# Image 2's expert sums move from TensorE to GpSimd, and two other moves in the tail of a fused attention and expert kernel

## The chip, the cores and the metric

One core of one Trainium2 chip runs the whole program. The metric is device time in microseconds (us) of one execution. TensorE (PE) multiplies matrices, VectorE (DVE), ScalarE (ACT) and GpSimd (POOL) work element by element, SyncE (SP) issues DMAs.

## What is computed

Four images of 64 channels and 1024 positions pass through an attention with projections, then a second attention on the normalized tokens, then a mixture of eight experts of which each token uses the two best. Cut to the last part, which the change touches:

```python
def _L1_ffn_ref(x, router_w, router_b, expert_w, expert_b):       # K = 2
    router_probs = jax.nn.softmax(x @ router_w + router_b, axis=-1)
    top_p, top_i = jax.lax.top_k(router_probs, K)
    top_p = top_p / jnp.sum(top_p, axis=-1, keepdims=True)
    expert_out = jnp.einsum('bnd,edc->bnec', x, expert_w) + expert_b
    gathered = jnp.take_along_axis(expert_out, top_i[..., None], axis=2)
    return jnp.einsum('bnk,bnkc->bnc', top_p, gathered)

t = t + _L1_attn_ref(_ln_t(t))
t = t + _L1_ffn_ref(_ln_t(t), router_w, router_b, expert_w, expert_b)
x = _from_tokens(t, x)
```

The kernel computes all eight experts for every token and multiplies each by a gate that is zero for six of them.

## The kernel before

Every engine has its own program, written out by hand in the order in which it runs; semaphores are the only link between them. Images 0 to 3 are staggered: while one image is in its first attention, the one ahead of it is in its second, and the experts of an earlier one run in between. Matmul results go into a ring of three PSUM buffers, in the order of the table ORDER; acc1 and acc2 are two further PSUM banks in which sums grow.

Tokens lie on partitions, 128 at a time, eight tiles to an image; two tiles are a pair, so an image has four pairs, g = 0 to 3. The steps that matter here, for image b:

- tokens2 (L1201, L1206) on VectorE turns the second attention's result into tok2; norm_stats (L1160 to L1171) takes the statistics of it; rstd on GpSimd (L370) raises the variances to the power -0.5; normalize2 (L1211) makes wn, the normalized tokens.
- w_transposed (L581) on TensorE turns wn, ScalarE rounds it into w_hi (L935), VectorE keeps the rest in w_lo (L1216); route (L594) makes the logits; top2 (L1224 to L1255) on VectorE picks two experts per token in some twenty small steps, each waiting for the one ahead, and ends in gate.
- experts (L605) multiplies a pair by all eight expert matrices into the ring; weigh_experts (L1266) multiplies that by the gates into prod, whose pair g is 128 x 1024: 8 experts x 2 tiles x 64 channels.
- For images 0 and 1 GpSimd adds the eight experts of a pair in three halving steps, sum_pair (L382, L384, L386: half, quart, ysum), and then residual and bias.
- For images 2 and 3, the tail, TensorE does the adding: start_sums (L624, L628) puts the turned tok2 and the turned expert bias into acc1 or acc2, and add_experts (L635) adds experts to them, each by one product with the identity, which turns it as well. Pair 0 of image 2 is added as eight experts; of pairs 1 to 3, and of pairs 0 to 2 of image 3, GpSimd first adds the upper four experts to the lower four in place (L421), so that TensorE adds four; the last pair is halved twice by VectorE (L1412, L1414) and TensorE adds two.
- GpSimd begins these in-place additions only behind a wait for s_w, that is for the wn of image 3.
- gates_transposed (L614) turns the gates, ScalarE copies them to gate_t (L943), and the bias products of start_sums wait for that. ScalarE copies the finished sums to ob (L1101 for image 2, L1105 and L1107 for the two halves of image 3), and SyncE stores them (L324, L330).

TensorE's order in the tail of before is: experts(2,1), experts(2,2), start_sums(2), add_experts(2,0), w_transposed(3), experts(2,3), route(3), experts(3,0) to (3,2), add_experts(2,1) to (2,3) with gates_transposed(3) ahead of the last of them, experts(3,3), start_sums(3) for pairs 0 and 1, their add_experts, start_sums(3) for pairs 2 and 3, and their add_experts.

Of the kernel before, what the change touches and what calls it, by code (L numbers as in the profile page):

```python
# [17 lines left out]
ALU = mybir.AluOpType  # L18
# [6 lines left out]
P = 128  # L25
B, C, N, M, E = 4, 64, 1024, 32, 8
CHUNK = 512
T = N // P
# [55 lines left out]
def build(nc, x, wq, wk, wv, wo, rw, rb, ew, eb, out):  # L84
    ctx = ExitStack()
    with ctx:
# [10 lines left out]
        ident = sb("ident", [P, P])  # L97
# [41 lines left out]
        ob = two("ob", [P, CHUNK])  # L139
# [29 lines left out]
        prod = sb("prod", [P, T // 2, E, 2, C])  # L169
        half = sb("half", [P, E // 2, 2, C])  # L170
        quart = sb("quart", [P, E // 4, 2, C])
        ysum = sb("ysum", [P, T, C])
# [124 lines left out]
        @block.sync  # L297
        def _(sp):
            def load_x(b):
                for h in range(2):  # L300
                    sp.dma_start(xin[h * C:(h + 1) * C, b, :], x[b].rearrange("c h w -> c (h w)")).then_inc(s_x[b], 16)

            first = x[0].rearrange("c h w -> c (h w)")
            for part in range(2):
                for h in range(2):
                    sp.dma_start(xin[h * C:(h + 1) * C, 0, chunk(part)], first[:, chunk(part)]).then_inc(s_x0[part], 16)
            sp.wait_ge(s_const, 1)
            for h in range(2):
                sp.dma_start(wo4[:, 2 * h, :], wo).then_inc(s_wol, 16)
            load_x(1)  # L310
            for h in range(2):
                sp.dma_start(e_in[h * C:(h + 1) * C, :, :], ew.rearrange("e d c -> d e c")).then_inc(s_ew, 16)
                sp.dma_start(r_in[h * C:(h + 1) * C, :], rw).then_inc(s_ew, 16)
            sp.dma_start(rb_all[:, :], rb.rearrange("(a e) -> a e", a=1).to_broadcast([P, E])).then_inc(s_ew, 16)
            for t in range(T):
                sp.dma_start(eb_in[t * E:(t + 1) * E, :], eb).then_inc(s_ew, 16)
            for b in range(2, B):
                load_x(b)

            flat_out = out.rearrange("b c h w -> (b c) (h w)")  # L320
            for b in range(B - 1):
                sp.wait_ge(s_ob, b + 1)
                for h in range(2):
                    sp.dma_start(flat_out[b * C:(b + 1) * C, chunk(h)], ob[b % 2][h * C:(h + 1) * C, :]).then_inc(s_out[b % 2], 16)  # L324
            b = B - 1
            for half_sum in range(2):
                sp.wait_ge(s_ob, B + half_sum)
                lo, hi = half_sum * CHUNK // 2, (half_sum + 1) * CHUNK // 2
                for h in range(2):
                    sp.dma_start(flat_out[b * C:(b + 1) * C, h * CHUNK + lo:h * CHUNK + hi],  # L330
                                 ob[b % 2][h * C:(h + 1) * C, lo:hi]).then_inc(s_out[b % 2], 16)
            sp.wait_ge(s_out[0], 2 * 32)
            sp.wait_ge(s_out[1], 3 * 32)
# [3 lines left out]
        def _(pool):  # L337
# [30 lines left out]
            def rstd(b, s_ve, s_rs, sm):  # L368
                pool.wait_ge(s_ve, b + 1)
                pool.tensor_tensor(sm[:, 3, :], sm[:, 2, :], minus_half[:, :], ALU.pow).then_inc(s_rs, 1)  # L370
                pool.wait_ge(s_rs, b + 1)
# [40 lines left out]
            rstd(3, s_ve1, s_rs1, sm1)  # L412
            experts(1)
            rstd(2, s_ve2, s_rs2, sm2)
            rstd(3, s_ve2, s_rs2, sm2)

            pool.wait_ge(s_w, B)
            for b, pairs in ((2, (1, 2, 3)), (3, (0, 1, 2))):
                for n, g in enumerate(pairs):
                    pool.wait_ge(s_prod, (T // 2) * b + g + 1)  # L420
                    pool.tensor_tensor(prod[:, g, 0:E // 2], prod[:, g, 0:E // 2], prod[:, g, E // 2:E],  # L421
                                       ALU.add).then_inc(s_half, 1)


        @block.tensor
        def _(pe):
# [194 lines left out]
            def start_sums(b, tiles, bank):  # L621

                for t in tiles:
                    pe.matmul(bank[:, t % len(tiles) * P:(t % len(tiles) + 1) * P],  # L624
                              tok2[b % 2][:, 2 * t:2 * t + 2, :].rearrange("p h c -> p (h c)"), ident[:, :],
                              start=(t == tiles[0]), stop=False)
                for t in tiles:
                    pe.matmul(bank[:, t % len(tiles) * P:(t % len(tiles) + 1) * P],  # L628
                              eb_blk[:, 2 * t:2 * t + 2, :].rearrange("p h c -> p (h c)"), gate_t[:, :],
                              start=False, stop=False)  # L630

            def add_experts(b, t, n, where, last):

                for e in range(n):
                    mm = pe.matmul(where, prod[:, t, e].rearrange("p h c -> p (h c)"), ident[:, :],  # L635
                                   start=False, stop=(last and e == n - 1))
                mm.then_inc(s_sums, 1)
# [214 lines left out]
            pe.wait_ge(s_tk2, 3)  # L852
            pe.wait_ge(s_gt, 3)
            start_sums(2, range(4), acc1)
            pe.wait_ge(s_prod, (T // 2) * 2 + 1)
            add_experts(2, 0, E, acc1[:, 0:P], False)
            w_transposed(3)
            experts(2, 3)
            route(3)
            experts(3, 0)  # L860
            experts(3, 1)
            experts(3, 2)
            for t in range(1, 4):
                pe.wait_ge(s_half, (T // 2) * 2 + t)
                add_experts(2, t, E // 2, acc1[:, t * P:(t + 1) * P], t == 3)
                if t == 2:
                    gates_transposed(3)
            experts(3, 3)
            pe.wait_ge(s_ob, 3)
            pe.wait_ge(s_tk2, B)  # L870
            pe.wait_ge(s_gt, B)
            start_sums(3, range(2), acc1)
            for t in range(2):
                pe.wait_ge(s_half, (T // 2) * 2 + 4 + t)
                add_experts(3, t, E // 2, acc1[:, t * P:(t + 1) * P], t == 1)
            start_sums(3, range(2, 4), acc2)
            pe.wait_ge(s_half, (T // 2) * 2 + 6)
            add_experts(3, 2, E // 2, acc2[:, 0:P], False)
            pe.wait_ge(s_tail_v, 2)
            add_experts(3, 3, E // 4, acc2[:, P:2 * P], True)  # L880
# [4 lines left out]
        def _(act):  # L885
# [219 lines left out]
            act.activation(ob[b % 2][:, 0:CHUNK // 2], acc1[:, 0:CHUNK // 2], ACT.Copy).then_inc(s_ob, 1)  # L1105
            act.wait_ge(s_sums, 8)
            act.activation(ob[b % 2][:, CHUNK // 2:CHUNK], acc2[:, 0:CHUNK // 2], ACT.Copy).then_inc(s_ob, 1)  # L1107


        @block.vector  # L1110
        def _(dve):
# [145 lines left out]
            def weigh_experts(b, g):  # L1257
                buf = filled(dve, f"e{g}", b)
                if g == 0:
                    dve.wait_ge(s_gate, b + 1)  # L1260
                if b in (1, 2):
                    dve.wait_ge(s_half, (T // 2) * (b - 1) + g + 1)
                if b == 3:
                    dve.wait_ge(s_sums, g + 1)
                gates = gate[b % 2][:, 2 * g:2 * g + 2, :].unsqueeze(3).to_broadcast([P, 2, E, C])
                dve.tensor_tensor(prod[:, g].rearrange("p e h c -> p h e c"), buf.rearrange("p h (e c) -> p h e c", c=C),  # L1266
                                  gates, ALU.mult).then_inc(s_prod, 1)
# [171 lines left out]
```

## Time and profile before

| what | value |
|---|---|
| device time, median of 3 runs | 212.69 us (212.67 to 213.76) |
| span of the profiled execution, first to last instruction | 211.2 us |
| what lies around the span (median less span) | some 1.5 us |
| TensorE busy | 197.3 us (93%) |
| VectorE busy | 144.4 us (68%) |
| ScalarE busy | 107.0 us (51%) |
| GpSimd busy | 62.0 us (29%) |
| TensorE clock granted over the span | 1.000 |

The page's busy rows by slices show TensorE at 7 to 9 tenths in nearly every slice, and GpSimd at 0 in nearly half of them; shares over the span say little about the last 25 us, though, where single steps wait for each other. The chain of waits says which they were. In the timeline a row gives start, duration, engine, line, operation, names, shapes and count, and in brackets how long the engine had been idle and who released it.

### The profile page before, as it was taken

To read this page: it belongs to the slowest core of one execution; us is meant where nothing else is said; L and a number is where in the kernel's file an instruction comes from. 1 tells how busy PE (TensorE), PEld (TensorE's weight loads), DVE (VectorE), ACT (ScalarE), POOL (GpSimd) and SP (SyncE) were. 2 spreads that over 40 slices of the span, in tenths; PEclk is the share of its full clock that TensorE was granted. 3 is DMA by queue.
4 is the path that set the end of the run, shared out by engine and by line. 5 is a ranking of instruction groups with operands and counts; after the bars stand their busy time and mean duration, and the time that the engine had idled before them with its cause. 6 is when DMAs were issued, how large, how long until landed. Compare 5 with 4: busy or idle time off the path is not lost.

```text
span 211.2 us, 3049 instructions
## 1 busy us (share of the span) xinstructions
PE 197.3 (93%) x1131; PEld 100.3 (47%) x1131; DVE 144.4 (68%) x359; ACT 107.0 (51%) x164; POOL 62.0 (29%) x75
## 2 busy tenths in 40 slices
PE   7999899899999899998989999899999999899993
PEld 2647443363734335453433545334435333387882
DVE  3889867978545994576489864827785362898980
ACT  3532776458655455576365636756555776301010
POOL 8140040403000300003003269710277770016270
PEclk9999999999999999999999999999999999999999
DMA  3853000000000000000000000020000002000021
GB/s 110 152 129 73 3 0 0 0 2 3 2 0 0 0 0 3 0 0 3 0 0 2 3 0 2 0 53 0 0 0 3 0 0 51 0 3 0 0 53 50
DMA packets 3502, 3.69 MB, mean 17 GB/s; under 512 B 2208, under 2 KB 2464, under 8 KB 3488
## 3 DMA queue, kind: packets, MB, share of 16 engines
q1 hardware_dynamic: 3248, 3.45, 7.2%
q8 instruction: 9, 0.15, 0.3%
q10 hardware_dynamic: 240, 0.05, 0.1%
q14 instruction: 5, 0.04, 0.1%
HBM read 2.45 MB, written 1.05 MB: 17 GB/s over the span
## 4 chain that ended last, share of the span: by engine, by line
PE 64%; DVE 26%; POOL 4%; issue 3%; ACT 2%; DVEq 0%; POOLq 0%
PE acc L494 19%; PE ring L558 9%; DVE rowmax L1127 8%; PE ring L605 6%; PE ring L487 5%; PE ring L469 5%; POOL sm L370 4%; PE acc L635 3%; PE acc L641 2%; PE ring L531 2%; DVE stats L1160 2%; PE ring L542 2%; PE ring L594 2%; DVE tok L1206 2%; PE ring L458 1%
## 5 line engine op out<-in xcount | busy, mean ns | idle before, releaser
L914 ACT ACTIVATE prob<-ring,shift 128x1024 f32<-128x1024 f32 x32 | 35.6, 1112 | 23.6 <-PE ring L558 23.3
L1127 DVE TENSOR_REDUCE rowmax<-ring 128x1 f32<-128x1024 f32 x32 | 38.1, 1219 | 12.5 <-PE ring L469 12.4
L370 POOL TENSOR_TENSOR sm<-sm,minus_half 128x8 f32<-128x8 f32 x8 | 15.8, 1974 | 99.7 <-DVE sm L1170 99.7
L911 ACT ACTIVATE prob<-ring 128x1024 f32<-128x1024 f32 x32 | 32.0, 1024 | 18.1 <-PE ring L487 18.0
L494 PE MATMUL acc<-prob,u 128*64 128x512 f32 x128 | 31.2, 606 | 0.2 <-ACT prob L914 0.2
L494 PE MATMUL acc<-prob,val 128*64 128x512 f32 x128 | 31.0, 605 | 0.0
L1266 DVE TENSOR_TENSOR prod<-ring,gate 128x1024 f32<-128x1024 f32 x16 | 19.3, 1220 | 6.8 <-PE ring L605 6.7
L487 PE MATMUL ring<-kst,qst 98*128 98x512 f32 x64 | 21.4, 425 | 1.1 <-DVE kst L1124 0.5
L469 PE MATMUL ring<-qst,kst 96*128 96x512 f32 x64 | 21.7, 429 | 0.7 <-DVE rowmax L1127 0.4
L558 PE MATMUL ring<-zsw,zst 64*128 64x512 f16 x64 | 19.4, 376 | 0.0
L558 PE MATMUL ring<-zst,zsw 64*128 64x512 f16 x64 | 19.2, 376 | 0.0
L487 PEld LDWEIGHTS ring<-kst,qst 98*128 98x128 f32 x64 | 10.4, 188 | 11.7 <-ACT prob L911 5.4
L494 PEld LDWEIGHTS acc<-prob,u 128*64 128x64 f32 x128 | 7.7, 136 | 15.6 <-issue 12.9
L494 PEld LDWEIGHTS acc<-prob,val 128*64 128x64 f32 x128 | 7.7, 136 | 15.2 <-issue 12.0
L469 PEld LDWEIGHTS ring<-qst,kst 96*128 96x128 f32 x64 | 10.2, 189 | 10.0 <-DVE rowmax L1127 4.0
L376 POOL TENSOR_TENSOR xst<-xin,xst 64x1024 fp32r<-64x1024 f32 x3 | 7.1, 2374 | 25.8 <-ACT xst L888 25.8
L382 POOL TENSOR_TENSOR half<-prod 128x512 f32<-128x512 f32 x8 | 10.6, 1322 | 8.4 <-DVE prod L1266 8.2
L558 PE MATMUL ring<-zst 64*128 64x512 f16 x32 | 12.3, 386 | 0.7 <-DVE rowmax L1127 0.4
L605 PE MATMUL ring<-e,w_hi 64*128 64x512 f32 x64 | 12.4, 443 | 0.0
L558 PE MATMUL ring<-zsw 64*128 64x512 f16 x32 | 12.4, 386 | 0.0
L605 PE MATMUL ring<-e,w_lo 64*128 64x512 f32 x64 | 10.9, 394 | 0.0
L641 PE MATMUL acc<-filler 128*128 128x512 f16 x21 | 7.9, 513 | 1.5 <-DVE filler L1270 1.5
(160 smaller groups left out, 323.8 us busy)
## 6 DMA issues: line engine op xcount, KB each, us to landing
xin<-in_x SPq DMA_DIRECT2D x6, 256.0 KB, 4.2
out<-ob SPq DMA_DIRECT2D x6, 128.0 KB, 2.4
xin<-in_x SPq DMA_DIRECT2D x4, 128.0 KB, 2.8
e_in<-in_L_ffn_expert_w SPq DMA_DIRECT2D x2, 128.0 KB
out<-ob SPq DMA_DIRECT2D x4, 64.0 KB, 2.0
eb_in<-in_L_ffn_expert_b SPq DMA_DIRECT2D x8, 2.0 KB
wo<-in_L_conv_wo SPq DMA_DIRECT2D x2, 8.0 KB, 2.2
r_in<-in_L_ffn_router_w SPq DMA_DIRECT2D x2, 2.0 KB
```

Of the source, the lines that this page charges most:

```text
L370: pool.tensor_tensor(sm[:, 3, :], sm[:, 2, :], minus_half[:, :], ALU.pow).then_inc(s_rs, 1)
L382: pool.tensor_tensor(half[:, :, :, :], p[:, 0:E // 2], p[:, E // 2:E], ALU.add).then_inc(s_half, 1)
L469: mm = pe.matmul(buf[:, h, :], kst[home][0:ROW, col(tile):col(tile) + P], qst[home][0:ROW, h * CHUNK:(h + 1) * CHUNK], start=True, stop=True)
L487: mm = pe.matmul(buf[:, h, :], qst[home][0:ROW + 2, col(j):col(j) + P], kst[home][0:ROW + 2, h * CHUNK:(h + 1) * CHUNK], start=True, stop= ...
L494: mm = pe.matmul(acc[h * C:(h + 1) * C, :], stationary[:, j, :], prob[:, j % DEEP, h * CHUNK:(h + 1) * CHUNK], start=(j == 0), stop=(j == ...
L558: mm = pe.matmul(buf[:, h, :], held[h][rows, col(j):col(j) + P], moving[h][rows, h * CHUNK:(h + 1) * CHUNK], start=(n == 0), stop=(n == 2))
L605: mm = pe.matmul(buf[:, h, :], w[rows, g * P:(g + 1) * P], e[rows, :], start=(n == 0), stop=(n == 3))
L641: pe.matmul(bank[:, :], filler[:, 0:P], filler[:, :], start=True, stop=True)
L911: act.activation(prob1[:, j % DEEP, :], flat(filled(act, f"st{j}", b)), ACT.Exp).then_inc(s_p1, 1)
L914: act.activation(prob2[:, j % DEEP, :], flat(filled(act, f"s{j}", b)), ACT.Exp, bias=shift[:, :], accum_out=rsum2[b % 2][:, j:j + 1]).then ...
L1127: dve.tensor_reduce(rowmax[:, tile:tile + 1], flat(filled(dve, f"mx{tile}", b)), AX.X, ALU.max).then_inc(s_mx, 1)
L1266: dve.tensor_tensor(prod[:, g].rearrange("p e h c -> p h e c"), buf.rearrange("p h (e c) -> p h e c", c=C), gates, ALU.mult).then_inc(s_pr ...
```

## The change

GpSimd's program: sum_pair for pair 0 of image 2 is put ahead of the last rstd, that of image 3, and sum_pair for pairs 1 to 3 behind it, in place of the three in-place additions of image 2; the wait for s_w is gone. The in-place additions for image 3 stay. GpSimd's end of program before, then after; names are those of the tiles above, sm is the statistics:

```order
L395 TENSOR_TENSOR y<-yres,ybias 128x512 [waits out_ready,ybias_ready,pool_step]
L370 TENSOR_TENSOR sm<-sm,minus_half 128x8 [waits var2_ready]
L370 TENSOR_TENSOR sm<-sm,minus_half 128x8 [waits var2_ready,rstd2_ready]
L421 TENSOR_TENSOR prod<-prod 128x512 [waits prods_ready,w_ready,rstd2_ready]
L421 TENSOR_TENSOR prod<-prod 128x512 [waits prods_ready] x5
```

```order
L370 TENSOR_TENSOR sm<-sm,minus_half 128x8 [waits var2_ready]
L382 TENSOR_TENSOR half<-prod 128x512 [waits prods_ready,rstd2_ready]
L384 TENSOR_TENSOR quart<-half 128x256 [waits prods_used]
L386 TENSOR_TENSOR ysum<-quart 128x128 [waits tree_step]
L370 TENSOR_TENSOR sm<-sm,minus_half 128x8 [waits var2_ready,tree_step]
L382 TENSOR_TENSOR half<-prod 128x512 [waits prods_ready,rstd2_ready]
L384 TENSOR_TENSOR quart<-half 128x256 [waits prods_used]
L386 TENSOR_TENSOR ysum<-quart 128x128 [waits tree_step]
L382 TENSOR_TENSOR half<-prod 128x512 [waits prods_ready,tree_step]
```

One sum_pair now stands between the two L370 of images 2 and 3, and three follow the second one with no wait for wn.

TensorE's program: add_experts(2,0) and the three other add_experts of image 2 are gone; a new add_sums adds the four ysum pairs, one product each, behind experts(3,2). gates_transposed(3) comes behind them, then a wait for gate_t and start_sums(3) for pairs 2 and 3 into acc2, and only then experts(3,3). TensorE from image 2's adding to image 3's first pair, before, then after:

```order
L635 MATMUL acc1<-ident,prod 128x128 [waits prods_used]
L635 MATMUL acc1<-ident,prod 128x128 x3
L614 MATMUL acc2<-ident,gate_1 128x128 [waits gates_ready,att2_read]
L635 MATMUL acc1<-ident,prod 128x128 [waits prods_used]
L635 MATMUL acc1<-ident,prod 128x128 x3
L605 MATMUL ring<-e1,w_hi_1 128x512 [waits prods_ready]
...
L624 MATMUL acc1<-ident,tok2_1 128x128 [waits gates_transposed,tok2_ready,out_ready]
```

```order
L636 MATMUL acc1<-ident,ysum 128x128 [waits tree_step] x4
L615 MATMUL acc2<-ident,gate_1 128x128 [waits gates_ready,att2_read]
L625 MATMUL acc2<-ident,tok2_1 128x128 [waits gates_transposed,tok2_ready]
L625 MATMUL acc2<-ident,tok2_1 128x128
L629 MATMUL acc2<-gate_t,eb_blk 128x128 x2
L606 MATMUL ring<-e1,w_hi_1 128x512 [waits prods_ready]
...
L625 MATMUL acc1<-ident,tok2_1 128x128 [waits out_ready]
```

The products for acc2 moved from behind image 3's first two pairs to ahead of experts(3,3), and with them the wait for gate_t.

VectorE's order is the same; weigh_experts of image 3 now waits for GpSimd's first halving of the same pair of image 2, where it waited for TensorE's adding of it. Of the last four stores SyncE issues three; ScalarE issues the last, of the lower half of the last sums, behind its own copy. The diff:

```diff
@@ sync: last stores @@
-                for h in range(2):
+                for h in range(2 - half_sum):
                     sp.dma_start(flat_out[b * C:(b + 1) * C, h * CHUNK + lo:h * CHUNK + hi],
@@ gpsimd: end of program @@
             rstd(2, s_ve2, s_rs2, sm2)
+            sum_pair(2, 0)
             rstd(3, s_ve2, s_rs2, sm2)
-            pool.wait_ge(s_w, B)
-            for b, pairs in ((2, (1, 2, 3)), (3, (0, 1, 2))):
-                for n, g in enumerate(pairs):
-                    pool.wait_ge(s_prod, (T // 2) * b + g + 1)
-                    pool.tensor_tensor(prod[:, g, 0:E // 2], prod[:, g, 0:E // 2], prod[:, g, E // 2:E],
-                                       ALU.add).then_inc(s_half, 1)
+            for g in range(1, T // 2):
+                sum_pair(2, g)
+
+            for g in range(T // 2 - 1):
+                pool.wait_ge(s_prod, (T // 2) * 3 + g + 1)
+                pool.tensor_tensor(prod[:, g, 0:E // 2], prod[:, g, 0:E // 2], prod[:, g, E // 2:E],
+                                   ALU.add).then_inc(s_half, 1)
@@ tensor @@
+            def add_sums(b, t, bank):
+                pe.wait_ge(s_tree, ((T // 2) * b + t) * 2 + 2)
+                pe.matmul(bank[:, t * P:(t + 1) * P], ysum[:, 2 * t:2 * t + 2, :].rearrange("p h c -> p (h c)"), ident[:, :],
+                          start=False, stop=(t == T // 2 - 1)).then_inc(s_sums, 1)
             start_sums(2, range(4), acc1)
-            pe.wait_ge(s_prod, (T // 2) * 2 + 1)
-            add_experts(2, 0, E, acc1[:, 0:P], False)
             w_transposed(3)
...
             experts(3, 2)
-            for t in range(1, 4):
-                pe.wait_ge(s_half, (T // 2) * 2 + t)
-                add_experts(2, t, E // 2, acc1[:, t * P:(t + 1) * P], t == 3)
-                if t == 2:
-                    gates_transposed(3)
+            for t in range(T // 2):
+                add_sums(2, t, acc1)
+            gates_transposed(3)
+            pe.wait_ge(s_tk2, B)
+            pe.wait_ge(s_gt, B)
+            start_sums(3, range(2, 4), acc2)
             experts(3, 3)
             pe.wait_ge(s_ob, 3)
-            pe.wait_ge(s_tk2, B)
-            pe.wait_ge(s_gt, B)
             start_sums(3, range(2), acc1)
...
-            start_sums(3, range(2, 4), acc2)
@@ scalar: end of program @@
+            act.wait_ge(s_ob, B + 1)
+            act.dma_start(out[b].rearrange("c h w -> c (h w)")[:, CHUNK + CHUNK // 2:N],
+                          ob[b % 2][C:P, CHUNK // 2:CHUNK]).then_inc(s_out[b % 2], 16)
@@ vector: weigh_experts @@
-                if b in (1, 2):
+                if b:
                     dve.wait_ge(s_half, (T // 2) * (b - 1) + g + 1)
-                if b == 3:
-                    dve.wait_ge(s_sums, g + 1)
```

## Rows read from the trace of the kernel before

**Rows 1.** Chain of waits, the tail: start us, us, what.

```profile
186.30 0.70 DVE tok L1206
...
189.14 1.96 POOL sm L370
...
191.19 0.70 DVE wn L1211
...
192.03 0.63 PE ring L581 x4
...
193.78 0.99 PE ring L594 x8
...
207.80 0.38 ACT ob L1107
```

**Rows 2.** Timeline of GpSimd and VectorE near 133 us (start, duration, instruction).

```profile
132.31 1.28 POOL L390 TENSOR_TENSOR yres<-ysum,tok 128x512 f32<-128x512 f32 x1
132.36 1.78 DVE L1206 TENSOR_TENSOR tok<-odiv,tok 128x512 f32<-128x512 f32 x1
133.67 1.60 POOL L395 TENSOR_TENSOR y<-yres,ybias 128x512 f32<-128x512 f32 x1
```

**Rows 3.** Timeline, VectorE beside GpSimd near 128 us; ring lies in PSUM.

```profile
128.13 1.23 DVE L1266 TENSOR_TENSOR prod<-ring,gate 128x1024 f32<-128x1024 f32 x1 [0.44 <-PE ring L605]
128.25 0.73 POOL L384 TENSOR_TENSOR quart<-half 128x256 f32<-128x256 f32 x1
```

**Rows 4.** Timeline of GpSimd, one sum_pair of image 0.

```profile
119.90 1.29 POOL L382 TENSOR_TENSOR half<-prod 128x512 f32<-128x512 f32 x1 [3.68 <-DVE prod L1266]
121.27 0.74 POOL L384 TENSOR_TENSOR quart<-half 128x256 f32<-128x256 f32 x1
122.08 0.46 POOL L386 TENSOR_TENSOR ysum<-quart 128x128 f32<-128x128 f32 x1
```

**Rows 5.** Timeline of VectorE and GpSimd, routing of images 2 and 3.

```profile
181.43 0.17 DVE L1234 TENSOR_TENSOR gm<-top 128x8 f32<-128x8 f32 x1
...
184.44 1.23 DVE L1266 TENSOR_TENSOR prod<-ring,gate 128x1024 f32<-128x1024 f32 x1
...
191.80 1.22 DVE L1266 TENSOR_TENSOR prod<-ring,gate 128x1024 f32<-128x1024 f32 x1
...
195.23 1.30 POOL L421 TENSOR_TENSOR prod<-prod 128x512 f32<-128x512 f32 x1 [0.69 <-DVE prod L1266]
...
196.31 0.24 DVE L1234 TENSOR_TENSOR gm<-top 128x8 f32<-128x8 f32 x1
...
196.79 0.29 DVE L1239 TENSOR_TENSOR cand<-cand,ramp 128x128 f32<-128x128 f32 x1
...
199.07 0.22 DVE L1255 TENSOR_TENSOR gate<-pick 128x64 f32<-128x64 f32 x1
```

**Rows 6.** Timeline of TensorE and ScalarE, from the gates of image 3 on.

```profile
199.59 0.27 PE L614 MATMUL acc<-ident,gate 128*128 128x128 f32 x1
...
199.90 0.27 ACT L943 ACTIVATE gate_t<-acc 64x128 f32<-64x128 f32 x1 [3.10 <-PE acc L614]
...
200.69 0.73 PE L605 MATMUL ring<-e,w_hi 64*128 64x512 f32 x4
```

**Rows 7.** Timeline of SyncE's queue, the last two stores.

```profile
208.21 0.47 SPq L330 DMA_DIRECT2D out<-ob  x1
...
208.72 0.60 SPq L330 DMA_DIRECT2D out<-ob  x1
```

**Rows 8.** Timeline of TensorE: start of the program, longest wait, image 2's sums.

```profile
6.25 0.74 PE L445 MATMUL ring<-xst,w 128*96 128x512 f32 x1
...
7.70 0.39 PE L445 MATMUL ring<-xst,w 128*96 128x512 f32 x1
...
42.58 0.88 PE L478 MATMUL ring<-ident_r,nmax 128*98 128x128 f32 x8 [1.04 <-DVE nmax L1135]
...
188.61 1.16 PE L628 MATMUL acc<-gate_t,eb_blk 64*128 64x128 f32 x8
```

More of the change, by code:

```diff
@@ L862, in _ @@
             experts(3, 2)
-            for t in range(1, 4):
-                pe.wait_ge(s_half, (T // 2) * 2 + t)
-                add_experts(2, t, E // 2, acc1[:, t * P:(t + 1) * P], t == 3)
-                if t == 2:
-                    gates_transposed(3)
+            for t in range(T // 2):
[4 more added lines that the diff above has]
+            start_sums(3, range(2, 4), acc2)
             experts(3, 3)
             pe.wait_ge(s_ob, 3)
-            pe.wait_ge(s_tk2, B)
-            pe.wait_ge(s_gt, B)
             start_sums(3, range(2), acc1)
             for t in range(2):
-                pe.wait_ge(s_half, (T // 2) * 2 + 4 + t)
+                pe.wait_ge(s_half, (T // 2) * 3 + t + 1)
                 add_experts(3, t, E // 2, acc1[:, t * P:(t + 1) * P], t == 1)
-            start_sums(3, range(2, 4), acc2)
-            pe.wait_ge(s_half, (T // 2) * 2 + 6)
+            pe.wait_ge(s_half, (T // 2) * 3 + 3)
             add_experts(3, 2, E // 2, acc2[:, 0:P], False)
```

## The prediction

> **What bounds the kernel now.** I read the page, then the chain of waits over the last 25 us, then the timelines of VectorE and GpSimd there, and last of the other stretches in which these two work at once. The chain is to show that the end is not set by TensorE's amount of work. It runs from VectorE's tok2 of image 3 (186.30) over GpSimd's power (189.14 to 191.10) back to VectorE's wn (191.19 to 191.89), through the turn and the routing products on TensorE (192.03, 193.78) to VectorE's pick of two experts, which ends in the gates at 199.07 + 0.22 = 199.29 [rows 1, 5]. From there the last copy starts 8.51 later, at 207.80 [rows 1]. So I cost the change as: when do the gates come, and how long is the way from the gates to the end.
>
> The timelines are to show how VectorE and GpSimd hold each other up. Near 133 us GpSimd starts an addition at 132.31, VectorE starts tok2, with both inputs in SBUF, 0.05 later, and takes 1.78 instead of the 0.69 to 0.70 of the tail: it ends at 134.14, 0.55 after GpSimd's end at 133.59. GpSimd's next addition, started at 133.67 while tok2 still runs, takes 1.60 instead of 1.28, as if it had begun 0.15 into its time and waited until 134.14 [rows 1, 2]. One waits for the whole instruction of the other. A VectorE instruction that reads the ring in PSUM is free of it: 1.23 beside GpSimd's 0.73, both their usual times [rows 3, 4]. Small ones are not free: L1234 takes 0.17 alone, and 0.24 where GpSimd's addition ran until 196.53; it ended just behind that, at 196.55 [rows 5]. In the tail of before, GpSimd's additions stay away from tok2, stand behind wn by a wait, and overlap the pick of experts in one instruction alone.
>
> **The change part by part.** The sum is made on the profiled execution, whose span of 211.2 lies 1.5 under the median; I add differences to 212.69.
>
> *sum_pair(2,0), ahead of the power.* Image 2's first weighing ends at 184.44 + 1.23 = 185.67 [rows 5]. GpSimd follows a VectorE result after about 0.14 (as TensorE follows wn: 191.89 to 192.03 [rows 1]), so half runs from 185.81 to 187.09 [1.28, rows 2, 4]. tok2 of image 3 starts at 186.30 in the middle of that, reads two SBUF tiles, and would end 0.55 behind it, at 187.64, not at 187.00: **+0.65** on the chain. quart (0.74) and ysum (0.46) are done near 188.8, a microsecond ahead of the power, now at 189.79; so the power waits for VectorE and not for them, and that part costs nothing.
>
> *sum_pair(2,1), with the wait for wn gone.* The power ends at 191.74. GpSimd's own next instruction follows it after 0.08 (121.19 to 121.27 [rows 4]), at 191.82, since its products are long there; VectorE's wn follows after 0.09 to 0.10 (191.10 to 191.19 [rows 1]), at 191.84. If GpSimd gets in first, as it did with 0.05 of lead in [rows 2], half ends at 193.10 and wn at 193.65, where it would have ended at 192.54: **+1.11**. The bounds are 0 and 1.28; I take GpSimd first, though the lead is 0.02. On this the Trainium skill speaks against the change: its page SBUF — State Buffer, section Who interferes with whom, says that issue order decides who blocks, for the whole instruction. By that page the lead alone decides, however small, and the sum is the one made here; rows 2 agree with a lead of 0.05, and no row here shows one of 0.02.
>
> *sum_pair(2,2) and (2,3), beside the pick of experts.* All of VectorE is now 0.65 + 1.11 = 1.76 late. GpSimd's quart of pair 1 waits for wn and ends at 194.23, its ysum at 194.77. Pair 2's products come at 191.80 + 1.22 + 1.76 = 194.78 [rows 5]; a sum_pair takes 1.28 + 0.73 + 0.46 and two gaps of 0.08, 2.63 in all [rows 4], so pair 2 runs from 194.92 to 197.55 and pair 3 from 197.63: half to 198.91, quart from 198.99 to 199.72, ysum to 200.26. L1234 would start at 196.31 + 1.76 = 198.07; it ends behind half, at 198.94 instead of 198.31: +0.63. L1239 would then start at 196.79 + 1.76 + 0.63 = 199.18, and is held by quart until 199.72: 0.40, since an instruction comes 0.14 into its time before it is held. The later small steps fall behind ysum's end. So **+1.03**; the bounds are 0 and the 2.63 for which pair 3 keeps GpSimd busy, and the row nearest is L1234's own. The gates come at 199.29 + 0.65 + 1.11 + 1.03 = 202.08.
>
> *TensorE.* add_experts(2,0) goes from a place where TensorE next waits for wn anyway: nothing gained. The other three of image 2, twelve products, become four, and the last ysum, at 200.26, is there 1.8 ahead of the gates; so TensorE has added them and waits when the gates come, and what counts is the way from there. New: turn of the gates 0.14 after them, 0.31 to ScalarE's copy, 0.27 for that, 0.14 back [rows 1, 6] = 0.86; then the work that stood in before from experts(3,3) at 200.69 to the last copy at 207.80, 7.11 [rows 1, 6], the same instructions in another order, with the acc2 products first. 7.97 instead of 8.51: **-0.54**. The new wait of TensorE for gate_t holds experts(3,3) behind it, which VectorE's fourth weighing wants: experts(3,3) ends about 0.86 + 1.2 + 1.1 = 3.2 after the gates, and VectorE comes to that weighing after three of 1.22, at 3.7. So it hides, with 0.5 in hand.
>
> *The last store.* SyncE issues its second store 0.51 behind the first [rows 7]; by ScalarE's queue both are issued at once. **-0.45**, between -0.51 and, if ScalarE's landed later, +0.3.
>
> *weigh_experts' new wait* is for halvings that end by 198.91, ahead of the gates: nothing.
>
> Sum: 0.65 + 1.11 + 1.03 - 0.54 - 0.45 = +1.80, so 212.69 + 1.80 = **214.5**.
>
> **The rivals.** *VectorE gets in first at wn.* The handovers differ by 0.02 only. wn is then not held, GpSimd's half waits for it (0.55), pairs 2 and 3 come 0.15 later than above and the pick of experts 1.11 earlier, so that more of its steps meet them. Going through it as above, L1239, L1242 and L1244 are held, 1.48 in all: gates at 201.42, +1.14, 213.8.
>
> *GpSimd does not hold VectorE.* If tok2, wn and the pick kept their times, because the rows near 133 had another cause, only the gains stay: -0.99, 211.7. That is the other side: not slower. It decides at tok2 and wn, and [rows 2] speak against it, in both directions at once.
>
> *TensorE's clock falls.* With add_experts(2,0) gone TensorE has nothing from 188.61 + 1.16 = 189.77 to wn's turn at 193.79: 4.0 idle. The longest wait of TensorE once it was under way was 1.04 [rows 8], and the page grants the full clock over the span. What the lower level costs shows at the start: L445 takes 0.74 before, and 0.39 once the clock is up [rows 8]. The turn and the routing products on the chain take 0.63 + 0.99 [rows 1]; doubled, they add 1.6, and up to 3 if the experts' products behind them wait too. I take +1.7: 216.2. The Trainium skill's page TensorE: Matmul & The Clock Gate, section Part 1: The HAM clock gate, says that an idle TensorE falls back to 1.2 GHz and must work to get 2.4 GHz again; no row of before shows a fall inside the program.
>
> **How the numbers follow.** GpSimd first at wn, clock kept: 0.50, 214.5. VectorE first: 0.23, 213.8. Clock falls: 0.16, 216.2. No holding, or much less of it: 0.11, 211.7 to 212.6. About 0.5% (1.06) is what a measurement of this kernel can tell from no change. The likeliest gives 214.5. The range takes in the first two with their bounds and half of the third: 213.1 to 216.3. Faster by over 0.5%: half of the case without holding, 0.05. Within 0.5%, up to 213.75: the rest of that and nearly half of VectorE first, 0.16. Slower: 0.79.
>
> **What would show it.** In the profile after: tok2 of image 3 at 1.3 instead of 0.69, with GpSimd's half under it; wn at 1.8, or half at 1.8 instead; L1234, L1239 or L1242 at 0.5 to 1.0; GpSimd busy from 191.8 to 200.3; the gates near 202; last copy 8.0 behind them; two stores issued at once. Wrong would be: VectorE's steps at their old lengths with GpSimd busy beside them; the last copy nearer to 8.5 behind the gates, which takes the TensorE term away; a granted clock under 1 after 193.

## The result

The changed kernel took 216.72 us (median of 4 runs, 215.08 to 217.27) where the kernel before, run beside it, took 212.68 (212.54 to 213.76). The ratio is 1.0161 (95% interval 1.0119 to 1.0204), which on 212.68 is 216.1. Slower was forecast, at 214.5 within 213.1 to 216.3. So the side is right and the ratio's value lies in the range, but the median of the runs lies 0.4 above it. The case taken as likeliest is not the one that happened: the rival of the falling clock is, to which 0.16 was given, and the range holds the value because it was drawn to take in half of that rival. That is luck more than judgement. Where a ratio is given, runs more than 1.5% above the fastest of the same kernel are left out of it; this concerns two of the ten of e2_gap.

Of the profiled execution (216.46 us) the page shows first where to look. These are its span, its row of TensorE's busy share in 40 slices, and the clock granted in the same slices:

```profile
span 214.7 us, 2998 instructions
...
PE   7999899899999899998989999899999999839994
...
PEclk9999999999999999999999999999999999985799
```

A slice is 5.4 us. TensorE is busy for 3 tenths of the slice that begins near 188, and in the next two slices the clock stands at 5 and 7 tenths. Before, this row held a 9 in every slice. Over the whole span the four executions were granted 0.976, 0.992, 0.976 and 0.976; the second, at 0.992, is the one of 215.08.

The stretches around it, TensorE's column and the granted clock above all (stretch, length, busy time and instructions of each engine, clock, share of the DMA engines, GB/s):

```profile
189.00:191.00 2.00, 0.76 (x7) 0.57 (x6) 1.93 (x7) 0.00 (x0) 1.23 (x1) 1.00 0.00 0
191.50:192.00 0.50, 0.00 (x0) 0.00 (x0) 0.16 (x1) 0.00 (x0) 0.42 (x2) 0.57 0.00 0
192.00:193.00 1.00, 0.00 (x0) 0.00 (x0) 1.00 (x1) 0.00 (x0) 1.00 (x1) 0.50 0.00 0
193.80:201.60 7.80, 7.80 (x34) 6.00 (x36) 5.52 (x20) 0.81 (x2) 5.82 (x8) 0.50 0.00 0
202.00:202.50 0.50, 0.50 (x8) 0.39 (x6) 0.47 (x4) 0.00 (x0) 0.00 (x0) 1.00 0.00 0
```

The clock falls to its lower level, 1.2 of 2.4 GHz, near 191.6, while TensorE waits. It stays there until shortly before 202, although TensorE worked through 7.80 of the 7.80 us up to 201.60.

Now the steps. VectorE in the stretch of [rows 1, 5] (start, duration, line, instruction, idle time before it and who released it):

```profile
186.27 1.36 DVE L1212 TENSOR_TENSOR tok<-odiv,tok 128x512 f32<-128x512 f32 x1
...
191.84 1.78 DVE L1217 TENSOR_TENSOR wn<-cen,sm 128x512 f32<-128x512 f32 x1 [0.48 <-POOL sm L370]
...
199.97 0.42 DVE L1240 TENSOR_TENSOR gm<-top 128x8 f32<-128x8 f32 x1
...
200.62 0.43 DVE L1245 TENSOR_TENSOR cand<-cand,ramp 128x128 f32<-128x128 f32 x1
...
203.03 0.23 DVE L1261 TENSOR_TENSOR gate<-pick 128x64 f32<-128x64 f32 x1
```

GpSimd beside it:

```profile
185.79 1.30 POOL L382 TENSOR_TENSOR half<-prod 128x512 f32<-128x512 f32 x1 [11.57 <-DVE prod L1270]
...
189.78 1.96 POOL L370 TENSOR_TENSOR sm<-sm,minus_half 128x8 f32<-128x8 f32 x1 [1.02 <-DVE sm L1176]
191.82 1.26 POOL L382 TENSOR_TENSOR half<-prod 128x512 f32<-128x512 f32 x1
...
199.62 0.74 POOL L384 TENSOR_TENSOR quart<-half 128x256 f32<-128x256 f32 x1
```

tok2 takes 1.36 where it took 0.70, wn 1.78 where it took 0.70 [rows 1], each with a half of GpSimd under it. At wn GpSimd was first, by 191.82 against 191.84: the 0.02 that had been worked out. The two steps of the pick (in the changed file L1240 and L1245, for L1234 and L1239 of before) take 0.42 and 0.43 instead of 0.24 and 0.29 [rows 5].

TensorE from image 2's bias products on, with ScalarE's three steps that belong to it in a fence of their own:

```profile
188.60 1.16 PE L629 MATMUL acc<-gate_t,eb_blk 64*128 64x128 f32 x8
193.77 1.09 PE L582 MATMUL ring<-ident,wn 128*128 128x128 f32 x4 [4.01 <-DVE wn L1217]
...
196.79 1.03 PE L595 MATMUL ring<-r_blk,w_hi 128*128 128x32 f32 x4
...
203.04 1.16 PE L636 MATMUL acc<-ident,ysum 128*128 128x128 f32 x8
204.04 0.27 PE L615 MATMUL acc<-ident,gate 128*128 128x128 f32 x1
204.76 0.68 PE L625 MATMUL acc<-ident,tok 128*128 128x128 f32 x4 [0.45 <-ACT gate_t L946]
```

```profile
204.35 0.27 ACT L946 ACTIVATE gate_t<-acc 64x128 f32<-64x128 f32 x1 [3.72 <-PE acc L615]
...
211.67 0.39 ACT L1110 ACTIVATE ob<-acc 128x256 f32<-128x256 f32 x1 [0.90 <-PE acc L642]
212.08 0.55 ACTq L1112 DMA_DIRECT2D out<-ob  x1
```

TensorE stands still for 4.01 us before wn's turn. The turn then takes 1.09 instead of 0.63 [rows 1]. The experts' products behind it run late too: the turned sums come at 203.04, after the work queued ahead of them, and so the gates, ready at 203.26, are turned only at 204.04.

Against the span of 211.2 the 3.5 us go as follows, step by step along the chain:

| step, after against before | forecast | measured |
|---|---|---|
| power starts at 189.78 instead of 189.14 (tok2 held) | +0.65 | +0.64 |
| wn ends at 193.62 instead of 191.89, less the above | +1.11 | +1.09 |
| first step of the pick at 199.97 instead of 196.31, less both (the clock) | 0 | +1.93 |
| gates at 203.26 instead of 199.29, less all three (pick held) | +1.03 | +0.31 |
| gates to the last copy, 8.41 instead of 8.51 | -0.54 | -0.10 |
| last copy to the end of the span, 3.0 instead of 3.4 | -0.45 | -0.4 |
| sum | +1.80 | +3.5 |

The first two lines are as forecast. The clock is the third: with the clock kept (e5_fill_both, below) the way from wn's end to the first step of the pick is 4.43, against 4.42 before; here it is 6.35. It also explains why the next two differ: with VectorE waiting for a slow TensorE, GpSimd's last pair is further along when the pick comes, and TensorE has a backlog when the gates come.

### The profile page after: what moved, and what is told of

Its sections match the earlier page's. It is cut to its first block, busy times and chain, and to the rows that moved or that the text cites. A ratio compares the mean times of both kernels' runs of the same rounds, so it can differ in the third digit from the quotient of the medians.

```text
span 214.7 us, 2998 instructions
## 1 busy us (share of the span) xinstructions
PE 197.0 (92%) x1099; PEld 99.2 (46%) x1099; DVE 146.5 (68%) x359; ACT 106.9 (50%) x164; POOL 68.8 (32%) x84
## 3 DMA queue, kind: packets, MB, share of 16 engines
q1 hardware_dynamic: 3168, 3.39, 6.5%
## 4 chain that ended last, share of the span: by engine, by line
PE 64%; DVE 26%; POOL 4%; issue 3%; ACT 2%; DVEq 0%; POOLq 0%
PE acc L495 18%; PE ring L559 8%; DVE rowmax L1133 8%; PE ring L606 7%; PE ring L488 5%; PE ring L470 4%; POOL sm L370 4%; PE acc L648 2%; PE ring L595 2%; PE ring L532 2%; DVE stats L1166 2%; PE ring L543 2%; DVE tok L1212 2%; PE acc L642 2%; DVE wn L1217 1%
## 5 line engine op out<-in xcount | busy, mean ns | idle before, releaser
L370 POOL TENSOR_TENSOR sm<-sm,minus_half 128x8 f32<-128x8 f32 x8 | 15.8, 1976 | 85.8 <-DVE sm L1176 85.8
L382 POOL TENSOR_TENSOR half<-prod 128x512 f32<-128x512 f32 x12 | 15.7, 1308 | 20.9 <-DVE prod L1270 20.7
L606 PE MATMUL ring<-e,w_hi 64*128 64x512 f32 x64 | 14.1, 490 | 0.0
L606 PE MATMUL ring<-e,w_lo 64*128 64x512 f32 x64 | 12.2, 431 | 0.0
L384 POOL TENSOR_TENSOR quart<-half 128x256 f32<-128x256 f32 x12 | 9.5, 794 | 0.9
```

The costliest lines, as they stand in the source:

```text
L382: pool.tensor_tensor(half[:, :, :, :], p[:, 0:E // 2], p[:, E // 2:E], ALU.add).then_inc(s_half, 1)
L384: pool.tensor_tensor(quart[:, :, :, :], half[:, 0:E // 4], half[:, E // 4:E // 2], ALU.add).then_inc(s_tree, 1)
L606: mm = pe.matmul(buf[:, h, :], w[rows, g * P:(g + 1) * P], e[rows, :], start=(n == 0), stop=(n == 3))
```

## The experiments

The theory after this reading: the forecast of 214.5 is what the change costs when the clock stays up, and everything above it is the clock, which falls because add_experts(2,0) is gone from TensorE's wait and because the new waits are longer. The rival: GpSimd's sums cost more than forecast in themselves, and the clock only goes along.

**One gap filled (e1_fill).** Products that nobody reads are put where TensorE waits for wn. keep_clock, a helper that the kernel before has and calls in its first 24 us alone, issues n products of 128x512 on constant data:

```diff
             start_sums(2, range(4), acc1)
+            keep_clock(17, acc2)
             w_transposed(3)
```

> The changed kernel with 17 dummy products of TensorE (128x512, result never read) behind start_sums of image 2, so that TensorE is not idle while wn is held. Theory: the change costs through two things, VectorE held by GpSimd (tok2 +0.65, wn +1.1, the pick of experts +1.0) and TensorE's clock, which falls in the 4.0 us gap. Then the clock stays at 1.00, the gates come near 202.1 and the time is 214.5 (214.2 to 214.8). Rival, the clock fall is harmless and the waits are all: 216.5 as without the dummies. Rival, the clock fall is all and the holding is hidden: 211.7 to 212.3.

It took 217.54 us (215.95 to 219.11, 4 runs; ratio 1.0216, 1.0138 to 1.0294): no gain at all. The windows tell why. The clock is kept through the filled gap and lost after 204:

```profile
189.00:201.00 12.00, 11.35 (x74) 7.22 (x73) 10.88 (x30) 0.81 (x2) 9.73 (x10) 1.00 0.00 0
...
204.00:205.00 1.00, 1.00 (x9) 0.64 (x6) 1.00 (x2) 0.00 (x0) 1.00 (x2) 0.68 0.69 160
205.00:207.00 2.00, 2.00 (x9) 1.38 (x7) 1.90 (x3) 0.00 (x0) 2.00 (x2) 0.50 0.25 59
```

TensorE's waits before that fall, and its last products behind it:

```profile
202.02 0.30 PE L615 MATMUL acc<-ident,gate 128*128 128x128 f32 x1 [1.42 <-DVE gate L1262]
202.77 0.68 PE L625 MATMUL acc<-ident,tok 128*128 128x128 f32 x4 [0.45 <-ACT gate_t L947]
...
207.70 5.04 PE L642 MATMUL acc<-ident,prod 128*128 128x128 f32 x28
```

With the clock up, TensorE is done early and waits 1.42 for the gates and 0.45 for their copy, which the change has put ahead of experts(3,3). The clock falls behind them, and the 28 last products take 5.04 (3.39 in the changed kernel, which has the full clock again by then). So the expectation failed, but the trace holds up to the gates what could not be seen in the changed kernel, the holding at full clock: tok2 1.35, wn 1.79, and in the pick

```profile
197.84 0.88 DVE L1241 TENSOR_TENSOR gm<-top 128x8 f32<-128x8 f32 x1
...
198.96 0.71 DVE L1246 TENSOR_TENSOR cand<-cand,ramp 128x128 f32<-128x128 f32 x1
```

which is 0.64 and 0.42 more than before, +1.06 against the +1.03 forecast. The gates end at 201.88. This execution runs 0.25 ahead (image 2's first weighing starts at 184.19 instead of 184.44), so they stand at 202.13 in the time of before; forecast 202.08.

**Both gaps filled (e5_fill_both).** To e1_fill is added:

```diff
                 add_sums(2, t, acc1)
+            keep_clock(6, acc2)
             gates_transposed(3)
```

> e1_fill with 6 more dummy products of TensorE behind the four turned sums, where it waited 1.4 us for the gates and where the clock fell in e1_fill. Theory: what e1_fill and the changed kernel lost beyond the holding is the clock alone, and short waits of TensorE suffice for it. Then the granted clock is 1.00 to the end, the gates come where they did in e1_fill, the last copy 8.0 behind them, the time is 214.5 (214.2 to 214.8). Rival, the dummies themselves or the new order cost the rest: 216 to 217.5 with the clock at 1.00.

It took 214.52 us (214.45 to 215.74, 6 runs; ratio 1.009, 1.0055 to 1.0124). The clock was 1.00 in four runs and 0.989 and 0.992 in two, which are the two above 215. In the profiled execution it stays up to the end:

```profile
190.00:200.00 10.00, 9.75 (x66) 6.25 (x63) 9.02 (x21) 0.81 (x2) 9.22 (x10) 1.00 0.00 0
200.00:212.00 12.00, 9.04 (x63) 6.82 (x61) 7.75 (x16) 1.52 (x4) 3.80 (x4) 1.00 0.19 45
```

The last copy, on ScalarE, and the gates it is measured from, on VectorE:

```profile
209.65 0.38 ACT L1112 ACTIVATE ob<-acc 128x256 f32<-128x256 f32 x1 [0.90 <-PE acc L642]
```

```profile
201.65 0.22 DVE L1263 TENSOR_TENSOR gate<-pick 128x64 f32<-128x64 f32 x1
```

From 201.87 to 209.65 are 7.78, against 8.51 before. So products that compute nothing take 2.2 us off the changed kernel's median, and what is left is the 214.5 worked out for a kept clock. The rival falls: the sums cost no more than forecast.

**The gap alone (e2_gap).** In the kernel before, TensorE adds one of the eight experts that it added while wn was awaited:

```diff
             pe.wait_ge(s_prod, (T // 2) * 2 + 1)
-            add_experts(2, 0, E, acc1[:, 0:P], False)
+            add_experts(2, 0, 1, acc1[:, 0:P], False)
```

> The kernel before, with one of eight experts added in add_experts(2,0), so that part of image 2's sum is left out: TensorE idles about 2.0 us there and nothing else moves. If a gap of that size already takes the clock down, the granted clock is 0.97 to 0.99, the turn of wn takes 1.1 instead of 0.63 and the time is 213.5 to 215. If it takes the 4 us gap that the holding makes, the clock stays at 1.00 and the time is 212.7, since the removed products lay in a wait.

Median 214.39 us (10 runs; ratio 1.0044, 0.9995 to 1.0093), but the median stands for neither kind of run: five took 212.65 to 213.13 with a clock of 0.999 or 1.00, five took 215.64 to 217.98 with 0.968 to 0.983, which is more than the 213.5 to 215 expected for a lost clock. GpSimd, VectorE and the waits are those of before. The profiled execution is one of the second kind. TensorE:

```profile
191.66 0.63 PE L581 MATMUL ring<-ident,wn 128*128 128x128 f32 x4 [1.82 <-DVE wn L1211]
...
193.86 1.03 PE L594 MATMUL ring<-r_blk,w_hi 128*128 128x32 f32 x4
```

and two of its windows:

```profile
193.00:196.00 3.00, 3.00 (x16) 2.31 (x14) 2.09 (x3) 0.00 (x0) 1.89 (x2) 0.50 0.00 0
...
200.00:204.00 4.00, 4.00 (x35) 3.42 (x35) 3.56 (x3) 0.73 (x2) 2.30 (x2) 1.00 0.00 0
```

Removing these products is by itself enough to lose the clock in half of the executions, with a wait of 1.82 us, and none of the change's sums on GpSimd is needed for it. The fall came when TensorE was already at work again, at about 192.7: the turn took its usual 0.63, where 1.1 was expected. Why five executions kept the clock and five lost it, these runs don't show.

**tok2's sum alone (e4_tok).** In the kernel before, GpSimd makes image 2's first sum ahead of the power, and nobody reads it (the counts of s_half in TensorE's waits go up by one, not shown):

```diff
             rstd(2, s_ve2, s_rs2, sm2)
+            sum_pair(2, 0)
             rstd(3, s_ve2, s_rs2, sm2)
```

> The kernel before, with one more sum_pair on GpSimd, that of pair 0 of image 2, ahead of image 3's power; its result is not used. Theory: tok2 of image 3 takes 1.3 instead of 0.69, the power starts 0.65 later, everything behind it too, the clock stays at 1.00: 213.3. Rival, GpSimd waits and not VectorE, or the delay is taken up later: 212.7.

It took 213.38 us (213.16 to 214.43, 10 runs; ratio 1.0032, 1.0015 to 1.0049): +0.69 for +0.65. VectorE's tok2, and TensorE's wait for wn with add_experts(2,0) still ahead of it:

```profile
185.96 1.36 DVE L1207 TENSOR_TENSOR tok<-odiv,tok 128x512 f32<-128x512 f32 x1
```

```profile
192.37 0.63 PE L582 MATMUL ring<-ident,wn 128*128 128x128 f32 x4 [0.94 <-DVE wn L1212]
```

The price of the holding at tok2 stands by itself here, with the clock granted at 0.992 or more in every run.

**The wait for wn put back (e3_wait_fill).** In the changed kernel, with 12 products in the gap, GpSimd's second pair waits for wn again:

```diff
             rstd(3, s_ve2, s_rs2, sm2)
+            pool.wait_ge(s_w, B)
             for g in range(1, T // 2):
```

> The changed kernel with the wait for wn put back ahead of sum_pair(2,1), and 12 dummy products in the gap. Theory of holding by whole instructions: wn takes 0.69 again and ends 1.1 earlier than in e1_fill, but the pairs of image 2 then meet more steps of the pick of experts (held 1.8 instead of 1.0): gates at 201.7, 214.1, only 0.4 under e1_fill. Rival, the hold at wn is the main cost and small steps are hardly held: 213.0 to 213.4.

It took 218.62 us (217.09 to 218.81, 4 runs; ratio 1.0251, 1.0203 to 1.03), 4.5 above what was expected, and again TensorE's column and the clock say why:

```profile
198.00:202.00 4.00, 1.77 (x11) 1.18 (x9) 3.70 (x12) 0.15 (x1) 2.23 (x3) 1.00 0.00 0
...
203.00:212.00 9.00, 9.00 (x39) 7.73 (x39) 4.28 (x5) 0.00 (x0) 3.55 (x3) 0.50 0.14 31
```

Up to the gates the theory of holding was right once more. wn takes 0.69 and is not held, and the pick meets GpSimd in two more steps than in e1_fill, the two below; all four together are held by 1.74, where 1.8 was expected:

```profile
198.14 0.99 DVE L1250 TENSOR_TENSOR pick<-cand,gm 128x64 f32<-128x64 f32 x1
199.17 0.76 DVE L1252 SCALAR_TENSOR_TENSOR cand<-pick,cand 128x64 f32<-128x64 f32 x1
```

The gates end at 201.37, 201.70 in the time of before (this execution runs 0.33 ahead); expected 201.7. Then waits of 1.46 for the last sum, 0.58 for the gates and 0.45 for their copy lose the clock, and all of the last 9 us are paid at the lower level. What the wait for wn is worth with the clock kept, this run doesn't show.

**The store alone (e6_store)**, in the kernel before:

```diff
-                for h in range(2):
+                for h in range(2 - half_sum):
...
             act.activation(ob[b % 2][:, CHUNK // 2:CHUNK], acc2[:, 0:CHUNK // 2], ACT.Copy).then_inc(s_ob, 1)
+            act.wait_ge(s_ob, B + 1)
+            act.dma_start(out[b].rearrange("c h w -> c (h w)")[:, CHUNK + CHUNK // 2:N],
+                          ob[b % 2][C:P, CHUNK // 2:CHUNK]).then_inc(s_out[b % 2], 16)
```

> The kernel before with nothing changed but the last store, which ScalarE issues. Theory: the two last stores are issued at once, -0.4: 212.3. Rival, the store by ScalarE lands later or the program's end does not hang on it: 212.7.

It took 212.48 us (212.27 to 213.62, 10 runs; ratio 0.9975, 0.9953 to 0.9997) where the kernel before, run beside it, took 212.78: -0.3 of the -0.45 forecast. The span ends 2.7 behind the last copy's end, at 207.93, instead of 3.0 behind it.

**The order as well (e7_store_order).** To e6_store is added the change's order, image 3's residual and bias for acc2 ahead of experts(3,3):

```diff
-            experts(3, 3)
-            pe.wait_ge(s_ob, 3)
             pe.wait_ge(s_tk2, B)
             pe.wait_ge(s_gt, B)
+            start_sums(3, range(2, 4), acc2)
+            experts(3, 3)
+            pe.wait_ge(s_ob, 3)
             start_sums(3, range(2), acc1)
...
-            start_sums(3, range(2, 4), acc2)
```

> e6_store with the acc2 products of image 3 ahead of experts(3,3), as in the change, but image 2's sums as before. TensorE has no idle time there in the kernel before, so the order alone brings nothing: 212.3 as e6_store. Rival, the wait for gate_t ahead of experts(3,3) delays VectorE's last weighing and the end: 212.6 to 213.

It took 211.97 us (211.90 to 214.18, 10 runs; ratio 0.9965, 0.9942 to 0.9988). By the medians that is 0.5 less than e6_store, by the ratios 0.2, by the fastest runs 0.4. The intervals of the two ratios overlap, so the times alone don't settle it. In the traces the gates come at 198.97 and the last copy starts at 207.10, 8.13 behind them where e6_store has 8.52. So the order brings something, against the expectation. TensorE shows what, in e6_store and then here:

```profile
200.44 0.73 PE L605 MATMUL ring<-e,w_hi 64*128 64x512 f32 x4
201.00 0.63 PE L605 MATMUL ring<-e,w_lo 64*128 64x512 f32 x4
...
202.21 0.71 PE L628 MATMUL acc<-gate_t,eb_blk 64*128 64x128 f32 x4
```

```profile
200.81 0.49 PE L628 MATMUL acc<-gate_t,eb_blk 64*128 64x128 f32 x2
201.03 0.50 PE L605 MATMUL ring<-e,w_hi 64*128 64x512 f32 x1
201.13 0.38 PE L628 MATMUL acc<-gate_t,eb_blk 64*128 64x128 f32 x2
201.28 0.71 PE L605 MATMUL ring<-e,w_hi 64*128 64x512 f32 x3
201.60 0.86 PE L605 MATMUL ring<-e,w_lo 64*128 64x512 f32 x4
202.39 0.71 PE L624 MATMUL acc<-ident,tok 128*128 128x128 f32 x4
```

The four bias products and the first four of the experts lie in each other's time: the first product of the experts starts at 201.03, ahead of the last bias products at 201.13. From the first bias product to what follows the experts' eight, 200.81 to 202.39, are 1.58 us. In e6_store the same twelve products stand apart and take 0.63 and 1.12, start to start, 1.75 together. Both kinds use 64 of the 128 rows: in the code the bias products read 64 partitions, and the experts' products by turns the first and the last 64. The Trainium skill's page TensorE: Matmul & The Clock Gate, section Part 3: Packing small matmuls — row/col tiling, says that products on different row groups of the array run at the same time; the rows agree. Which half a record used, the rows don't say. From the first of this work to the last copy are 6.83 us, against 7.11 in e6_store: 0.17 less through the overlap, and 0.10 less because the 28 last products stand in one run (3.43 to the last copy, against 1.89 and 1.64 in two).

**A version that beats both (e8_quart).** To e7_store_order is added that GpSimd halves image 3's first pair a second time, so that TensorE adds two products of it, and not four:

```diff
+                    if b == 3 and g == 0:
+                        pool.wait_ge(s_half, (T // 2) * 2 + 4)
+                        pool.tensor_tensor(prod[:, g, 0:E // 4], prod[:, g, 0:E // 4], prod[:, g, E // 4:E // 2],
+                                           ALU.add).then_inc(s_tree, 1)
...
-                add_experts(3, t, E // 2, acc1[:, t * P:(t + 1) * P], t == 1)
+                add_experts(3, t, E // 4 if t == 0 else E // 2, acc1[:, t * P:(t + 1) * P], t == 1)
```

> e7_store_order, and GpSimd halves pair 0 of image 3 a second time, behind the gates, where VectorE weighs from PSUM and is not held; TensorE then adds two experts of that pair instead of four. Theory: TensorE sets the end there, so 0.4 of its work comes off: 211.9. VectorE's two last halvings may be held by GpSimd (up to 0.7), which TensorE reaches later anyway. Rival, that holding decides: 212.3 or more.

It took 211.79 us (211.57 to 213.02, 12 runs; ratio 0.9955, 0.9937 to 0.9974), less than either kernel. Its last copy starts 7.75 behind the gates, 0.38 less than in e7_store_order. (Its profiled execution, 212.95, was granted a lower clock in the fourth of 40 slices, 15.8 to 21.1 us, so only differences are read in it.) VectorE's halving of the last pair is held by GpSimd's two last halvings. In e7_store_order, and here with GpSimd beside it:

```profile
203.77 0.88 DVE L1415 TENSOR_TENSOR prod<-prod 128x512 f32<-128x512 f32 x1
```

```profile
205.16 1.71 DVE L1422 TENSOR_TENSOR prod<-prod 128x512 f32<-128x512 f32 x1
```

```profile
203.83 2.48 POOL L421 TENSOR_TENSOR prod<-prod 128x512 f32<-128x512 f32 x2
```

It takes 1.71 instead of 0.88. But TensorE's products are queued until then, so the end still comes earlier: here the holding costs nothing, since nobody waits for the held engine.

## Why the prediction was right and wrong

*tok2, +0.65, and wn, +1.11: right.* Measured +0.64 and +1.09 in the changed kernel, and the first of them alone +0.69 in e4_tok. At wn GpSimd had a lead of 0.02, in the changed kernel and in e5_fill_both alike (191.58 against 191.60 there), and that lead decided. On this the Trainium skill's page SBUF — State Buffer, section Who interferes with whom, was right: issue order decides, and for the whole instruction. So the rival in which VectorE gets in first did not happen, nor did the one without holding.

*The pick of experts, +1.03: right for a kept clock.* +1.06 in e1_fill and +1.07 in e5_fill_both, in the two steps named, the first 0.88 to 0.90 and the second 0.70 to 0.71. In the changed kernel itself it was +0.31, since the clock moved the pick away from GpSimd's last pair.

*TensorE's way from the gates, -0.54: mis-sized, on the safe side, and given back.* With the clock kept it is 7.78 instead of 8.51, -0.73. Turn and copy of the gates took 0.90 as costed (0.86), but the work behind took 6.88 and not 7.11: mainly because the twelve products of bias and experts took 1.56 instead of 1.75, lying in each other's time, and the 28 last 3.43 instead of 3.53. "The same instructions in another order" was costed as the same time. In the changed kernel 8.41 were measured, 0.63 more than 7.78: its gates are turned 0.78 after they are there, behind TensorE's backlog, and 0.15 after in e5_fill_both.

*The last store, -0.45:* -0.4 in the changed kernel's trace, -0.3 in e6_store.

*add_experts(2,0), "nothing gained": the step that failed.* Its removal was costed at nothing because it lay in a wait. It gained nothing, but it cost something: those products were work that stood between TensorE and a lower clock. The prediction saw the 4.0 us of idle time (4.01 measured) and the clock as a rival, and gave that 0.16, since no row of before showed a fall inside the program. Where a resource is not seen to fail in the trace of before, though, the trace of before is no witness for a wait four times as long as its longest, 1.04 [rows 8]; and the kernel before fills waits near its start itself, by keep_clock. e2_gap shows a fall in half of its executions after 1.82. In the changed kernel three of four executions were granted 0.976; the fourth's 0.992 says less, since the kernel before was granted 0.992 in 7 of the 50 executions that have a clock on record, and never less. The holding has its part in the wait: with add_experts(2,0) kept, some 2.0 would have been left (0.28 before, and 0.64 + 1.09; an estimate), as much as in e2_gap. No run has that case.

*The rival's price, +1.7, 216.2: near, with parts that cancel.* It was made from the turn and the routing products, doubled; the doubling came from L445 at the start of the program [rows 8]. The granted clock of that stretch is 1.00 in the trace of before, so that row doesn't show a lower level by the clock; the changed kernel's rows do. There, at a clock of 0.50, the turn took 1.01 instead of 0.56 from start to start, experts(2,3) behind it 2.01 instead of 1.12 and the routing products 1.81 instead of 1.00: less than double each, but three and not two, 2.15 together, of which some 0.2 were hidden, because before VectorE was still weighing when the routing products ended. So that term came out at +1.93 where 1.6 was worked out; with it go 0.72 less for the pick and 0.44 less gain on TensorE's way, 1.65 together. So the profiled execution has the 3.5 that the rival had as 1.8 + 1.7.

*One more part was missed, and the result did not show it:* with one gap filled the next one takes its place. The prediction saw TensorE waiting for the gates and costed this wait as time that hides. e1_fill and e3_wait_fill lose the clock there, with 1.42 + 0.45 and 1.46 + 0.58 + 0.45 of waiting, and end later than the changed kernel by their medians.

So of the change, the store and the order gain (0.7 together in e7_store_order, by its ratio), and GpSimd's sums of image 2 and what they take out of TensorE lose all that and more.

## What to carry to other kernels

Products that lie in a wait are not free to remove: before taking work out of TensorE's waits, look at every wait that remains along the path, not at the longest alone, and price the products behind them at the lower clock. An engine that relieves TensorE by sums in SBUF holds VectorE up for whole instructions, so its work belongs beside VectorE steps that read PSUM, or where nobody waits for VectorE. And when products use half of the array's rows, what stands next to them in the program can be worth something of its own, here some 0.2 us.

## What the hardware showed that was not expected

- *The clock is lost to short waits, and can be lost late.* In e1_fill and e2_gap it fell when TensorE was back at work: after 204, with waits that ended at 202.02 and 202.77, and at about 192.7, with a wait that ended at 191.66. The waits in the tail and the clock granted over the whole span in all runs of each kernel:

| kernel | waits of TensorE from 189 on until the gates are copied | clock |
|---|---|---|
| the kernel before, e6_store, e7_store_order, e8_quart | 0.28 each | more than 0.992 in 71 of 82, 0.992 in ten, 0.984 in one (of e7_store_order) |
| e4_tok | 0.94 | 0.997 or more in 9 of 10, 0.992 in one |
| e5_fill_both | 0.25, 0.45 | 1.00 in 4 of 6, 0.989 and 0.992 in two |
| e2_gap | 1.82 | 0.999 or more in 5 of 10, 0.968 to 0.983 in 5 |
| e1_fill | 0.24, 1.42, 0.45 | 0.975 to 0.984 in 3 of 4, 0.991 in one |
| e3_wait_fill | 0.22, 1.46, 0.58, 0.45 | 0.975 to 0.984 in 4 of 4 |
| the changed kernel | 4.01, 0.45 | 0.976 in 3 of 4, 0.992 in one |

  A clock of 0.984 or less stands in 15 of the 22 executions of the last four kernels, and in one of the 98 others. Only one execution of each kernel has a trace, so where a run at 0.989 to 0.992 lost it is not known; in e8_quart's it was near the start of the program, and the kernel before has such runs too.

- *Once lost, it does not come back soon.* In the changed kernel the lower level lasted from 191.6 to near 202, over 7.8 us of work without a pause; in e2_gap from about 192.7 to 199.5. The executions of e2_gap that lost it took 2.5 to 5.3 us longer than those that kept it.
- *Even a step of 128 x 8 elements is held like a large one:* 0.17 alone, 0.88 behind GpSimd's half in e1_fill.
- *Products on 64 rows overlap across instructions of different kinds*, as e7_store_order shows: twelve of them took 1.58 us instead of 1.75 by a change of order alone.
